# Attention and expert layer on one core: value products of neighbouring items side by side, three weight buffers, values projected at the end of the turn

## Chip, cores, metric

One NeuronCore of a Trainium2 chip. The metric is the device time of one execution, in microseconds (us). The profiler's names of the engines: PE is TensorE's matrix products (PEld its weight loads), DVE VectorE, ACT ScalarE, POOL GpSimd, SP the engine that issues DMAs here.

## What is computed

x has 16 batch items of 1024 tokens by 256. Attention has 16 heads of 16 dimensions, with rotary positions on q and k and a causal mask; then a gated mixture of 8 experts, the two best of each token.

```python
qkv = x @ W_qkv;  q, k, v = split(qkv);  q, k = rope(q, k)
att = einsum('bhtd,bhsd->bhts', q, k) / sqrt(16) + causal_mask
y = einsum('bhts,bhsd->bhtd', softmax(att), v) @ W_o
x = layernorm(x + y)
gate = softmax(x @ Wg + bg);  keep the two largest of 8, divide by their sum
out = layernorm(x + sum over experts of gate * (x @ We.T + be))
```

## The kernel before

The kernel works on one batch item per **turn**. Everything that a turn does is cut into steps, and one table, `ORDER`, writes all steps of a turn in a row; each engine runs its own part of each step in that order, and semaphores connect the engines. `plan(seg)` filters the table for five segments: `pre` (projection and first maxima of the first batch item), `first`, `mid` (14 turns), `last`, and `post` (the rest of the last item's expert layer). A middle turn does three things at once: attention of its own item, projection of the next item, expert layer of the item before.

- `ST.n.h`: scores of item n (0 to 47), head h of four, a bf16 product of up to 512 columns into one of NS = 3 PSUM tiles `scores` (line 963). ACT takes the exponential into `weights[:, n % 2]` (line 642). An *item* is one block of 128 keys by up to 512 queries for four heads; a slot of four heads has 12 items, whose widths are 512, 384, 256, 128 for the first four, then four of 512 and again 512, 384, 256, 128.
- `MASK.n`: on a diagonal item POOL sets weights above the diagonal to zero (line 559). 
- `PV.n`: the value product of item n. Four f32 products, one head each, with stationary values of 128 by 32; each goes to its own 32 partitions of `attend` (line 983). A f32 product stands in the trace as two passes, so one PV is eight records. PV.n stands after ST.n+1, since there are two weight buffers: the exponentials of item n+2 wait for PV.n (`attended`).
- `B.s.it.h`: the same scores the other way round, for the row maxima (line 947); DVE takes the maximum out of one of NB = 4 PSUM banks (lines 760, 763). `MC`, `MT` gather the maxima of a slot, which go by DMA into the stack for the next turn.
- `VP.j`: values of the next item for two token tiles (line 936), four steps a turn; ACT copies them into `v_next` (line 628). `VCOPY.s`: POOL copies slot s from `v_next` to `v_now` (line 584), when the slot's last value product is done.
- `XL`, `XT`: SP loads the next item's x in four pieces into `x_in` (line 472), PE transposes it (line 915). `QK`, `ROPE`, `CAST`, `LOAD` make the stacks of q and k.
- `YE`, `YT`, `HT`, `WO`: output of attention. `ZT`, `GL`, `GLT`, `GA`, `GB`, `GT`, `BE`, `MOE` (line 890): gating and experts; `BE.g.0`, `BE.g.1` are the products with the experts' bias (line 1045), whose contraction has 8 rows. `N1A`, `N2`, `R1`, `R2`, `N2A`: the norms; after `N2A` SP stores the result (line 518) and at the turn's end waits until the store has landed (line 522), before it issues `XL.0` of the next turn.

Of the kernel before, what the change touches and what calls it, by code (L numbers as in the profile page):

```python
# [38 lines left out]
NS = 3  # L39
DMA = 16  # L40
# [3 lines left out]
CONST_P, CONST_V = 4, 3  # L44
# [38 lines left out]
def item_work(n):  # L83
# [7 lines left out]
XL.0  # L91
ST.0.0 ST.0.1 ST.0.2 ST.0.3 XL.1 B.0.0.0 B.0.0.1 MC.3 B.0.0.2 B.0.0.3 MASK.0 PV.47 YE.3.1
ST.1.0 ST.1.1 B.0.1.0 ST.1.2 B.0.1.1 B.0.1.2 YT.3.1 ST.1.3 MASK.1 PV.0 B.0.1.3 B.0.2.0
ST.2.0 XT.0 B.0.2.1 XL.2 XT.1 B.0.2.2 ST.2.1 ST.2.2 XL.3 XR.0 ST.2.3 MASK.2 MT.3 B.0.2.3 PV.1
ST.3.0 ST.3.1 B.0.3.0 B.0.3.1 VCOPY.3 ST.3.2 ST.3.3 XR.1 MASK.3 B.0.3.2 PV.2
ST.4.0 ST.4.1 XT.2 XT.3 HT.0.0 HT.0.1 ST.4.2 ST.4.3 B.0.3.3 LOAD.0 B.0.4.0 B.0.4.1 PV.3 YE.0.0
ST.5.0 B.0.4.2 WO.0.0 WO.0.1 HT.1.0 HT.1.1 B.0.4.3 QK.0.0 ST.5.1 R1.0 ST.5.2 ST.5.3 WSPLIT B.0.5.0 B.0.5.1
  B.0.5.2 PV.4 ROPE.0.0
ST.6.0 B.0.5.3 B.0.6.0 B.0.6.1 ST.6.1 ST.6.2 ST.6.3 PV.5 B.0.6.2 B.0.6.3
ST.7.0 ST.7.1 B.0.7.0 B.0.7.1 CAST.0.0.0 QK.0.1 B.0.7.2 ST.7.2 CAST.0.0.1 ST.7.3 B.0.7.3 B.0.8.0 PV.6  # L100
ST.8.0 ROPE.0.1 N1A.0 WO.1.0 B.0.8.1 WO.1.1 ST.8.1 ST.8.2 ST.8.3 MASK.8 PV.7 B.0.8.2
ST.9.0 ST.9.1 B.0.8.3 B.0.9.0 CAST.0.1.0 QK.0.2 YT.0.0 B.0.9.1 ST.9.2 B.0.9.2 ST.9.3 MASK.9 R1.1 PV.8
# [52 lines left out]
def belongs(step, seg):  # L155
# [6 lines left out]
    if step in (("PV", SLOTS * ITEMS - 1), ("YE", SLOTS - 1, 1), ("YT", SLOTS - 1, 1)):  # L162
        return behind
# [925 lines left out]
```

## Time and profile before

| | |
|---|---|
| median of 3 runs | 3425.34 us (3417.21 to 3430.62) |
| the profiled execution's own time | 3433.1 us |
| its span | 3431.4 us |
| busy, share of the span | PE 96%, DVE 80%, ACT 55%, POOL 36% |
| mean granted TensorE clock | 0.975 of full |

The span is from the first to the last instruction. The 14 middle turns are alike, some 204.5 us each. Before them lie some 120 us of `pre` and the segment `first`, behind them `last` and some 110 us of `post`.

### The profile page before, as it was taken

What the parts mean: (1) busy time and instruction counts of PE and PEld (TensorE: products, weight loads), DVE (VectorE), ACT (ScalarE), POOL (GpSimd) and SP (SyncE); (2) the same over time, 40 slices, a digit from 0 to 9 for tenths busy, and PEclk for the clock granted to TensorE, in tenths of its full rate; (3) what the DMA queues carried; (4) which work ended last, traced back from release to release, by engine and by line L of the source; (5) the groups of instructions that cost most, each with busy time, mean ns of one, the idle gap of its engine ahead of it and who ended that gap; (6) DMA issues with size and microseconds to landing.
All of it is one profiled execution on the core that took longest, in us unless ns stands there. A gap on an engine that the chain in (4) does not pass through costs nothing.

```text
span 3431.4 us, 59169 instructions
## 1 busy us (share of the span) xinstructions
PE 3291.5 (96%) x19072; PEld 1738.4 (51%) x19072; DVE 2741.6 (80%) x8349; ACT 1897.2 (55%) x4257; POOL 1234.4 (36%) x1467
## 2 busy tenths in 40 slices
PE   5899999999999999999999999999999999999987
PEld 2234555555555555555555555555555555555555
DVE  5778887878888788888878888787888878888735
ACT  2367555564655556555564655657465564655541
POOL 4254324343333444334344332444334344432110
PEclk7799999999999999999999999999999999999998
DMA  5334343232433333343242433333343242434000
GB/s 135 59 61 81 52 84 56 45 79 48 83 52 68 59 58 70 52 84 57 50 79 42 83 57 74 57 55 69 58 78 57 52 75 50 77 52 72 2 25 13
DMA packets 174790, 210.98 MB, mean 61 GB/s; under 512 B 25992, under 2 KB 124560, under 8 KB 174224
## 3 DMA queue, kind: packets, MB, share of 16 engines
q1 hardware_dynamic: 173056, 202.98, 33.9%
q8 instruction: 153, 2.51, 0.4%
q10 hardware_dynamic: 1424, 4.21, 0.3%
q14 instruction: 157, 1.29, 0.2%
HBM read 138.43 MB, written 67.11 MB: 60 GB/s over the span
## 4 chain that ended last, share of the span: by engine, by line
PE 81%; DVE 9%; issue 3%; POOL 2%; DMA 2%; ACT 1%; DVEq 0%; ACTq 0%; SPq 0%; POOLq 0%
PE bank L890 22%; PE attend L983 15%; PE bank L947 13%; PE scores L963 13%; PE bank L927 6%; PE bank L1007 3%; PE bank L1045 2%; DVE bank L760 2%; PE bank L936 2%; DMA x_in<-in_x 2%; PE bank L991 1%; DVE maxima L763 1%; PE bank L915 1%; PE bank L998 1%; PE bank L1015 1%
## 5 line engine op out<-in xcount | busy, mean ns | idle before, releaser
L642 ACT ACTIVATE weights<-scores 128x512 f32<-128x512 f32 (+3 forms) x3072 | 1351.6, 494 | 1077.5 <-PE scores L963 1067.2
L760 DVE CUSTOM_DVE_ANT_0 bank<-bank,far_q 128x128 f32<-128x128 f32 (+3 forms) x2048 | 960.6, 514 | 217.2 <-PE bank L947 200.4
L963 PE MATMUL scores<-q_stack,k_stack 99*128 99x512 bf16 (+3 forms) x3072 | 826.1, 330 | 8.6 <-ACT weights L642 8.3
L947 PE MATMUL bank<-k_stack,q_stack 96*128 96x512 bf16 (+3 forms) x3072 | 792.6, 334 | 31.7 <-DMA k_stack<-parts_scratch 8.9
L559 POOL TENSOR_SCALAR_AFFINE_SELECT weights<-weights 128x512 f32<-128x512 f32 x512 | 325.3, 637 | 1201.7 <-ACT weights L642 1199.8
L763 DVE TENSOR_REDUCE maxima<-bank 128x1 f32<-128x512 f32 x1024 | 641.9, 682 | 49.0 <-PE bank L947 43.6
L983 PE MATMUL attend<-weights,v_now 128*32 128x512 f32 (+3 forms) x6144 | 660.9, 502 | 3.9 <-POOL weights L559 3.8
L963 PEld LDWEIGHTS scores<-q_stack,k_stack 99*128 99x128 bf16 x3072 | 265.7, 98 | 526.2 <-ACT weights L642 275.4
L947 PEld LDWEIGHTS bank<-k_stack,q_stack 96*128 96x128 bf16 x3072 | 271.2, 98 | 480.3 <-issue 242.2
L864 DVE SCALAR_TENSOR_TENSOR z<-bank,gates,z 128x256 f32<-128x256 f32 x512 | 247.0, 482 | 204.9 <-PE bank L890 203.6
L890 PE MATMUL bank<-wexp_hi,zT_hi 128*128 128x512 f32 x1024 | 377.2, 450 | 0.0
L890 PE MATMUL bank<-wexp_lo,zT_hi 128*128 128x512 f32 x1024 | 327.5, 401 | 0.0
L890 PE MATMUL bank<-wexp_hi,zT_lo 128*128 128x512 f32 x1024 | 325.9, 400 | 0.0
L927 PE MATMUL bank<-xT,wqkv_sb 128*128 128x512 f32 x512 | 248.4, 609 | 21.3 <-DVE z L866 13.9
L866 DVE SCALAR_TENSOR_TENSOR z<-bank,gates,z 128x256 f32<-128x256 f32 x512 | 247.9, 484 | 18.3
L983 PEld LDWEIGHTS attend<-weights,v_now 128*32 128x32 f32 x6144 | 121.6, 108 | 222.2 <-issue 171.9
L890 PEld LDWEIGHTS bank<-wexp_lo,zT_hi 128*128 128x128 f32 x1024 | 197.5, 193 | 47.3
L890 PEld LDWEIGHTS bank<-wexp_hi,zT_lo 128*128 128x128 f32 x1024 | 195.8, 191 | 47.4
L569 POOL TENSOR_SCALAR shrink<-moments 128x4 f32<-128x4 f32 x64 | 15.0, 234 | 561.2 <-DVE moments L878 388.9
L890 PEld LDWEIGHTS bank<-wexp_hi,zT_hi 128*128 128x128 f32 x1024 | 185.3, 196 | 53.6 <-issue 19.2
L548 POOL TENSOR_TENSOR rope<-rope,cos_sb 128x512 f32<-128x512 f32 x128 | 165.3, 1292 | 122.7 <-DVE rope_swap L789 122.6
L617 ACT ACTIVATE parts<-rope 128x512 bf16<-128x512 f32 x256 | 162.0, 633 | 60.5 <-POOL rope L552 30.8
(106 smaller groups left out, 3467.2 us busy)
## 6 DMA issues: line engine op xcount, KB each, us to landing
parts_scratch<-parts SPq DMA_DIRECT2D x128, 384.0 KB, 2.5
q_stack<-parts_scratch SPq DMA_DIRECT2D x384, 128.0 KB, 7.1
k_stack<-parts_scratch SPq DMA_DIRECT2D x384, 128.0 KB, 7.6
x_in<-in_x SPq DMA_DIRECT2D x64, 256.0 KB, 3.0
z<-in_x SPq DMA_DIRECT2D x32, 512.0 KB, 5.1
out<-z SPq DMA_DIRECT2D x32, 512.0 KB, 3.4
q_stack<-maxrow SPq DMA_DIRECT2D x192, 8.0 KB, 2.1
z<-in_w_exp ACTq DMA_DIRECT2D x1, 1024.0 KB, 14.5
```

The source lines that it names most:

```text
L548: pool.tensor_tensor(x1, x1, cos[:, ch * CH:(ch + 1) * CH], ALU.mult)
L559: pool.affine_select(out=block, in_=block, compare_op=ALU.is_ge, fill=no_weight, base=0, pattern=[[0, QUAD], [1, P]], channel_multiplier=- ...
L642: act.activation(weights[:, n % 2, hh, c0:CH], st[(QUAD * n + hh) % NS][:, c0:CH], ACT.Exp, scale=DH ** -0.5).then_inc(S["weights_ready"], 1)
L760: dve.tensor_tensor_reduce(out=b[:, 0:w], in0=b[:, 0:w], in1=far_q[:, CH - w:CH], scale=1.0, scalar=-SENTINEL, op0=ALU.add, op1=ALU.max, a ...
L763: dve.tensor_reduce(dst, b[:, 0:w], AX.X, ALU.max).then_inc(fr, 1)
L864: link(c, step, dve.scalar_tensor_tensor(out=acc, in0=b[:, 0:D], scalar=gates[:, t, 2 * ch:2 * ch + 1], in1=acc, op0=ALU.mult, op1=ALU.add))
L866: dve.scalar_tensor_tensor(out=acc, in0=b[:, D:2 * D], scalar=gates[:, t, 2 * ch + 1:2 * ch + 2], in1=acc, op0=ALU.mult, op1=ALU.add).then ...
L890: last = pe.matmul(dst, lhs(i, kt), rhs(j, kt), start=(i, j, kt) == pairs[0], stop=(i, j, kt) == pairs[-1])
L927: last = pe.matmul(b[:, :], wqkv[:, kt, col:col + P], xT[:, kt, ch * CH:(ch + 1) * CH], start=kt == 0, stop=kt == KT - 1)
L947: pe.matmul(b[:, 0:w], q_stack[0:ROWS, n, hh, qt * P:(qt + 1) * P], k_stack[0:ROWS, n, hh, kc * CH:kc * CH + w], start=True, stop=True).th ...
L963: pe.matmul(st[(QUAD * n + hh) % NS][:, c0:CH], k_stack[0:MROWS, s, hh, kb * P:(kb + 1) * P], q_stack[0:MROWS, s, hh, qc * CH + c0:(qc + 1 ...
L983: last = pe.matmul(pv[32 * j:32 * j + 32, c0:CH], v_now[:, s, o:o + 32], weights[:, n % 2, j, c0:CH], start=kb == 0, stop=kb == 4 * qc + 3)
```

## The change

Three buffers hold weights (`NW = 3`), so PV.n may stand one item later; the table puts PV.2m and PV.2m+1 next to each other, after ST.2m+2 and the mask. `v_next` and `v_now` become one tile `values` of five places. Slots 0 to 2 of the next item are projected straight into the places 1 to 3 that the products read, and slot 3 into place 4, from which POOL copies it to place 0 (one copy a turn in place of four). So VP can run only when slots 0 to 2 have been used: it stands at ST.45 to ST.47, at the end of the turn. The last two value products of an item (46, 47) run in the next turn, before only the last one did. Two small tiles of the gating are reused in place. The table of all steps is written anew; two lines of it before and after:

```diff
+NW = 3
-ST.15.0 ST.15.1 ST.15.2 GT.0 VP.3 ST.15.3 CAST.0.3.0 MASK.15 B.1.2.2 PV.14 B.1.2.3 B.1.3.0
-ST.16.0 ST.16.1 BE.0.0 ST.16.2 ST.16.3 B.1.3.1 CAST.0.3.1 B.1.3.2 B.1.3.3 PV.15 YE.1.0
+ST.15.0 B.1.2.1 MT.0 ST.15.1 ST.15.2 BE.0.0 BE.0.1 B.1.2.2 MOE.0.0.0 ST.15.3 B.1.2.3 B.1.3.0 MASK.15
+ST.16.0 ST.16.1 MOE.0.0.1 CAST.0.3.0 ST.16.2 B.1.3.1 B.1.3.2 MOE.0.0.2 B.1.3.3 ST.16.3 PV.14 PV.15 YE.1.0
...
-    if step in (("PV", SLOTS * ITEMS - 1), ("YE", SLOTS - 1, 1), ("YT", SLOTS - 1, 1)):
+    if step in (("PV", SLOTS * ITEMS - 2), ("PV", SLOTS * ITEMS - 1), ("YE", SLOTS - 1, 1), ("YT", SLOTS - 1, 1)):
...
-        v_next = sb("v_next", [P, SLOTS, VQ])
-        v_now = sb("v_now", [P, SLOTS, VQ])
+        values = sb("values", [P, SLOTS + 1, VQ])
-        weights = sb("weights", [P, 2, QUAD, CH])
+        weights = sb("weights", [P, NW, QUAD, CH])
...
                 elif kind == "VCOPY":
-                    (s,) = a
-                    if s < SLOTS - 1:
-                        emptied(pool, c, ("VP", TILES // 2 - 1))
-                    if c.seg != "pre" and (c.seg != "first" or s < SLOTS - 1):
-                        pool.wait_ge(S["attended"], c.at("attended", ("PV", ITEMS * s + ITEMS - 1)))
+                    projected(pool, c)
+                    if c.seg != "first":
+                        pool.sem_inc(S["pool_waits"], 1)
+                        pool.wait_ge(S["attended"], c.at("attended", ("PV", SLOTS * ITEMS - 1)))
                     pool.sem_inc(S["pool_waits"], 1)
-                    pool.tensor_copy(v_heads(v_now, s), v_heads(v_next, s)).then_inc(S["values_copied"], 1)
+                    pool.tensor_copy(v_heads(0), v_heads(SLOTS)).then_inc(S["values_copied"], 1)
...
                         act.wait_ge(S["values_copied"], c.at("values_copied", ("VCOPY", SLOTS - 1)))
+                        act.wait_ge(S["attended"], c.at("attended", ("PV", ITEMS * (SLOTS - 1) - 1)))
...
-                        if n >= 2:
-                            act.wait_ge(S["attended"], c.at("attended", ("PV", n - 2)))
+                        if n >= NW:
+                            act.wait_ge(S["attended"], c.at("attended", ("PV", n - NW)))
...
-                        last = pe.matmul(pv[32 * j:32 * j + 32, c0:CH], v_now[:, s, o:o + 32],
-                                         weights[:, n % 2, j, c0:CH], start=kb == 0, stop=kb == 4 * qc + 3)
+                        last = pe.matmul(pv[32 * j:32 * j + 32, c0:CH], values[:, (s + 1) % SLOTS, o:o + 32],
+                                         weights[:, n % NW, j, c0:CH], start=kb == 0, stop=kb == 4 * qc + 3)
```

What PE runs in a middle turn around the bias products `BE` (line 1045; 1047 after), before:

```order
L1045 MATMUL bank<-narrow 128x256 x2
L963 MATMUL scores<-q_stack,k_stack 128x512 x2
L947 MATMUL bank<-k_stack,q_stack 128x512 x3
L983 MATMUL attend<-weights,v_now 32x128 x4
L963 MATMUL scores<-q_stack,k_stack 128x512
L947 MATMUL bank<-k_stack,q_stack 128x512
L963 MATMUL scores<-q_stack,k_stack 128x512
L947 MATMUL bank<-k_stack,q_stack 128x512
L963 MATMUL scores<-q_stack,k_stack 128x512
L1045 MATMUL bank<-narrow 128x256 x2
L890 MATMUL bank<-wexp_hi,zT_hi 128x512 x2
```

and with the change:

```order
L963 MATMUL scores<-q_stack,k_stack 128x256 x2
L947 MATMUL bank<-k_stack,q_stack 128x384
L985 MATMUL attend<-weights,values 32x512 x4
L985 MATMUL attend<-weights,values 32x384 x4
L963 MATMUL scores<-q_stack,k_stack 128x128
L947 MATMUL bank<-k_stack,q_stack 128x384
L953 MATMUL bank<-ident,maxima 32x128
L963 MATMUL scores<-q_stack,k_stack 128x128 x2
L1047 MATMUL bank<-narrow 128x256 x4
```

The two bias products stand together (x4), no longer with eight rows between them, and the row of value products (line 985 after) is a pair, 512 and 384 wide, where before each stood alone between other products.

What PE runs at the passage from one turn to the next (line 915 is XT, the transposition of the x that SP loads; lines 983 and 985 are the value products), before, from PV.46 on:

```order
L983 MATMUL attend<-weights,v_now 32x256 x4
L963 MATMUL scores<-q_stack,k_stack 128x512 x4
L947 MATMUL bank<-k_stack,q_stack 128x128 x4
L983 MATMUL attend<-weights,v_now 32x128 x4
L963 MATMUL scores<-q_stack,k_stack 128x384 x2
L947 MATMUL bank<-k_stack,q_stack 128x256
L963 MATMUL scores<-q_stack,k_stack 128x384
L947 MATMUL bank<-k_stack,q_stack 128x256 x2
L991 MATMUL bank<-ident,head_out 128x128 x4
L963 MATMUL scores<-q_stack,k_stack 128x384
L983 MATMUL attend<-weights,v_now 32x512 x4
L947 MATMUL bank<-k_stack,q_stack 128x256
```

and with the change, from the last value projection (VP.3, line 936) on:

```order
L936 MATMUL bank<-wqkv_sb,xT 128x256 x4
L963 MATMUL scores<-q_stack,k_stack 128x128 x2
L947 MATMUL bank<-k_stack,q_stack 128x512
L915 MATMUL bank<-ident,x_in 128x128 x8
L947 MATMUL bank<-k_stack,q_stack 128x128 x2
L963 MATMUL scores<-q_stack,k_stack 128x512 x2
L947 MATMUL bank<-k_stack,q_stack 128x128 x2
L947 MATMUL bank<-k_stack,q_stack 128x256 x2
L963 MATMUL scores<-q_stack,k_stack 128x512 x2
L947 MATMUL bank<-k_stack,q_stack 128x256
L985 MATMUL attend<-weights,values 32x256 x4
L985 MATMUL attend<-weights,values 32x128 x4
```

The first transposition of the next item's x stood further down, among the scores of the third item; now it is the first thing of the turn, behind the value projections.

In a middle turn the step table has 24 pairs of value products. Of these 23 follow each other on PE with nothing between; PV.18 and PV.19 have maxima products between them.

## Rows read from the trace of the kernel before

**Rows 1.** The page: busy time, share of the span, instructions of each engine.

```profile
PE 3291.5 (96%) x19072; PEld 1738.4 (51%) x19072; DVE 2741.6 (80%) x8349; ACT 1897.2 (55%) x4257; POOL 1234.4 (36%) x1467
```

**Rows 2.** The page: the chain that ended last, by engine and by line.

```profile
PE 81%; DVE 9%; issue 3%; POOL 2%; DMA 2%; ACT 1%; DVEq 0%; ACTq 0%; SPq 0%; POOLq 0%
PE bank L890 22%; PE attend L983 15%; PE bank L947 13%; PE scores L963 13%; PE bank L927 6%; PE bank L1007 3%; PE bank L1045 2%; DVE bank L760 2%; PE bank L936 2%; DMA x_in<-in_x 2%; PE bank L991 1%; DVE maxima L763 1%; PE bank L915 1%; PE bank L998 1%; PE bank L1015 1%
```

**Rows 3.** Windows: length, busy us (instructions), clock, DMA; one turn, then two short stretches.

```profile
core 0: us, PE busy (x) PEld busy (x) DVE busy (x) ACT busy (x) POOL busy (x), PEclk, DMA share, GB/s
1511.03:1715.50 204.47, 201.82 (x1196) 107.79 (x1192) 169.57 (x521) 118.36 (x267) 77.67 (x92) 0.99 0.37 63
1658.99:1662.40 3.41, 3.41 (x17) 1.84 (x16) 2.98 (x8) 0.66 (x3) 0.63 (x1) 1.00 0.03 5
1662.40:1665.80 3.40, 3.40 (x16) 2.06 (x15) 2.03 (x7) 2.92 (x7) 2.72 (x3) 0.50 0.02 5
```

**Rows 4.** Waits of PE, 300 to 3200 us: total us, times, longest.

```profile
PE bank L927 <- DVE z L866: 13.9, 14, 1.0
PE bank L1037 <- DVE gates L849: 12.5, 14, 0.9
PE scores L963 <- ACT weights L642: 4.7, 16, 0.7
PE bank L915 <- DMA x_in<-in_x: 3.8, 8, 0.8
```

**Rows 5.** Timeline of PE around one group of value products (start us, us, line).

```profile
1499.85 0.82 PE L963 MATMUL scores<-q_stack,k_stack 99*128 99x512 bf16 x3
1500.60 0.64 PE L983 MATMUL attend<-weights,v_now 128*32 128x512 f32 x4
...
1501.06 0.61 PE L983 MATMUL attend<-weights,v_now 128*32 128x512 f32 x4
1501.60 0.39 PE L963 MATMUL scores<-q_stack,k_stack 99*128 99x512 bf16 x1
1501.83 0.38 PE L947 MATMUL bank<-k_stack,q_stack 96*128 96x512 bf16 x1
```

**Rows 6.** Timeline of PEld, the same stretch.

```profile
1499.85 0.33 PEld L963 LDWEIGHTS scores<-q_stack,k_stack 99*128 99x128 bf16 x3 [0.28 <-issue]
1500.60 0.16 PEld L983 LDWEIGHTS attend<-weights,v_now 128*32 128x32 f32 x8 [0.42 <-issue]
1501.60 0.10 PEld L963 LDWEIGHTS scores<-q_stack,k_stack 99*128 99x128 bf16 x1 [0.84 <-ACT weights L642]
```

**Rows 7.** Timeline of PE around the two bias products of one half.

```profile
1659.22 0.22 PE L963 MATMUL scores<-q_stack,k_stack 99*128 99x128 bf16 x1
1659.38 1.13 PE L1045 MATMUL bank<-narrow 8*128 8x256 f32 x4
1660.43 0.60 PE L947 MATMUL bank<-k_stack,q_stack 96*128 96x512 bf16 x2
1660.88 0.22 PE L963 MATMUL scores<-q_stack,k_stack 99*128 99x128 bf16 x1
1661.03 1.13 PE L1045 MATMUL bank<-narrow 8*128 8x256 f32 x4
```

**Rows 8.** Page and timeline: the end of a turn, out of ACT and SP.

```profile
1505.87 2.08 ACT L676 ACTIVATE z<-z,shrink 128x256 f32<-128x256 f32 x4
...
1507.97 0.40 SPq L518 DMA_DIRECT2D out<-z  x1
1511.03 7.86 SPq L472 DMA_DIRECT2D x_in<-in_x  x4
...
x_in<-in_x SPq DMA_DIRECT2D x64, 256.0 KB, 3.0
```

**Rows 9.** Groups of PE by line: busy us, mean ns (value projection).

```profile
L936 PE MATMUL bank<-wqkv_sb,xT 128*128 128x256 f32 x512 | 121.4, 381 | 4.6 <-ACT rope L607 3.3 <-ACT v_next L628 0.9 <-DVE maxima_hi L760 0.5
```

**Rows 10.** Timeline of DVE from the gates' first step to the last.

```profile
1567.77 0.28 DVE L834 MAX8 top<-logits 128x8 f32<-128x8 f32 x3
...
1572.90 0.19 DVE L849 TENSOR_TENSOR gates<-chosen,gate_sum 128x32 f32<-128x32 f32 x1
```

**Rows 11.** Timeline of SP at the start of the first item.

```profile
119.63 1.77 SPq L510 DMA_DIRECT2D q_stack<-maxrow  x3
121.44 6.01 SPq L472 DMA_DIRECT2D x_in<-in_x  x4
```

**Rows 12.** The page: groups of ACT and DVE that feed or free PE.

```profile
L642 ACT ACTIVATE weights<-scores 128x512 f32<-128x512 f32 (+3 forms) x3072 | 1351.6, 494 | 1077.5 <-PE scores L963 1067.2
L760 DVE CUSTOM_DVE_ANT_0 bank<-bank,far_q 128x128 f32<-128x128 f32 (+3 forms) x2048 | 960.6, 514 | 217.2 <-PE bank L947 200.4
...
L763 DVE TENSOR_REDUCE maxima<-bank 128x1 f32<-128x512 f32 x1024 | 641.9, 682 | 49.0 <-PE bank L947 43.6
```

More of the change, by code:

```diff
@@ L146 @@
[L146 to L151 removed]
+XL.0 XL.1 XT.0 XL.2 XT.1 XL.3 B.0.0.0 B.0.0.1 MC.3
@@ L195, in plan @@
                 out += [("LOAD", 1)]
-        out += [("VCOPY", s) for s in range(SLOTS - 1)]
         out += [("LOAD", 2)] + scores + [("MC", 0), ("MT", 0)]
@@ L413, in attention_moe_kernel, with v_heads, projected @@
         free = [sem(f"bank{i}_free") for i in range(NB)]
-        def v_heads(buf, s):
-            return buf[:, s, 0:TILES * QUAD * VW].rearrange("p (b h v) -> p b h v", b=TILES, h=QUAD)
+        def v_heads(place):
+            return values[:, place, 0:TILES * QUAD * VW].rearrange("p (b h v) -> p b h v", b=TILES, h=QUAD)
+        def projected(eng, c):
+            before = {"first": ("pre",), "last": ("mid", NMID - 1)}.get(c.seg)
+            if c.seg == "mid":
+                before = ("mid", c.turn - 1) if c.turn else ("first",)
+            emptied(eng, Count(*before), ("VP", TILES // 2 - 1))
         def filled(eng, c, step):
@@ L557, in work @@
                     pool.wait_ge(S["weights_ready"], c.at("weights_ready", ("ST", n, QUAD - 1)))
-                    block = weights[:, n % 2, :, c0:c0 + P]
+                    block = weights[:, n % NW, :, c0:c0 + P]
                     pool.affine_select(out=block, in_=block, compare_op=ALU.is_ge, fill=no_weight, base=0,
@@ L845, in work @@
                     dve.wait_ge(S["gate_exp"], c.at("gate_exp", ("GA", a[0])))
-                    link(c, step, dve.tensor_tensor(chosen[:, :, :], gate_e[:, :, :], picked[:, :, :], ALU.mult))
-                    link(c, step, dve.tensor_reduce(gate_sum[:, 0], chosen[:, :, :], AX.X, ALU.add))
+                    link(c, step, dve.tensor_tensor(picked[:, :, :], shift[:, :, :], picked[:, :, :], ALU.mult))
+                    link(c, step, dve.tensor_reduce(gate_sum[:, 0], picked[:, :, :], AX.X, ALU.add))
                     link(c, step, dve.reciprocal(gate_sum[:, 1], gate_sum[:, 0]))
-                    dve.tensor_tensor(gates[:, :, :], chosen[:, :, :],
+                    dve.tensor_tensor(gates[:, :, :], picked[:, :, :],
                                       gate_sum[:, 1].unsqueeze(2).to_broadcast([P, 4, NE]), ALU.mult) \
@@ L970, in work @@
                     c0 = score_width(kb, qc)
-                    if it == 0:
+                    if n == 0:
+                        projected(pe, c)
+                    elif n == ITEMS * (SLOTS - 1):
                         pe.wait_ge(S["values_copied"], c.so_far("values_copied", step))
```

131 lines of the change are left out of this document (62 added, 69 removed).

## Prediction

> **What bounds the kernel.** I read the page's first part, then its chain, then one middle turn, then PE's waits, and last the single records. TensorE is busy 96% of the span, no other engine over 80% [rows 1], and the chain that ended last lies on it for 81%, 15% on the value products alone [rows 2]. A middle turn lasts 204.47 us, of which PE is busy 201.8; VectorE 169.6 and ScalarE 118.4 [rows 3]. From 300 to 3200 us PE's named waits come to under 30 us in all, two of which come once a turn: 1.0 us for a bank that VectorE frees late (13.9 us) and 0.9 us for the gates (12.5 us) [rows 4]. So only what shortens PE's own stream shortens the kernel, and "busy" hides one thing: what PE loses between products.
>
> That loss shows in the starts [rows 5]. Three score products start at 1499.85, and in an undisturbed stream each next 512-wide one starts 0.22 later (1501.60 to 1501.83 is 0.23). So the third starts at about 1500.29, and the value product behind it at 1500.60, 0.31 later: 0.09 lost on entering. Inside the group the second pass starts 0.46 after the first. From the second pass to the next score product it is 0.54: 0.08 lost on leaving. The weight loads tell the same [rows 6]: three score weights are loaded within 0.33, ahead of their products, but the first load for the value product starts only at 1500.60, with the product, and the next full-width load only at 1501.60. Each change between full-width products and 32-column products costs PE 0.08 to 0.09 us.
>
> **The pairs.** Before, each of the 768 value products is entered and left alone. The new order puts 23 pairs a turn together, 16 times: 368 passages from a value product to a full-width one and back are gone. The trace has no passage from one item's value product to the next item's (the price of it is unknown); the nearest row is the passage between the two passes of one group, 0.46, which has the same kind of product, the same 32-column places and a fresh load of weights each time [rows 5, 6]. If the passage between items is like it, a pair saves 0.09 + 0.08 = 0.17 us. The other end is a passage that drains as the outer ones do: 0. Below 0 nothing speaks, as the second item now waits for weights that are an item older. I take 0.175, since the starts are rounded and the sum of the two may be 0.17 or 0.18: 368 x 0.175 = **64 us** (bounds 0 and 66).
>
> **The bias products.** They have the same kind of loss: a 128-wide score product (0.06 in a stream) starts at 1659.22 and the bias product at 1659.38, 0.10 late, and leaving is much like it [rows 7]. Two of them a half now stand together, in two halves of 16 turns: 32 x 0.18 = **6 us** (bounds 0 and 6).
>
> **Waits that go or come.** The 1.0 us wait for VectorE stood at a projection whose bank the expert product before it had used while VectorE was busy with a row of maxima; in the new order this projection (QK.1.1) has a pair of value products and a maxima product between it and the last user of its bank, 2 us of cover: **-14 us** (bounds 0 and 14). The gates: VectorE needs 5.3 us from the first step to the last, 1567.77 to 1573.09 [rows 10]. In the new order some 4 us of PE work lie between GA and the transposition GT, with two maxima products that VectorE takes in between, and VectorE starts GA about as PE comes to it; so PE waits again, 5.3 - 4 = 1.3 to 1.4 us in place of 0.9: **+5 us** (bounds -12 and +15).
>
> **x at the head of the turn.** The transposition XT.0 is now the first work of a turn. What it needs: ScalarE's last normalization, 2.08 us, the store of its result, from issue to the next load's issue 3.06 us, and the load, 3.0 us to landing [rows 8]. The normalization now stands behind the first exponential of item 46, say 0.8 us after PE began that item; with it the data is there 8.9 us after the first score product of item 46. Between the two points PE now has three value projections (121.4 us / 64 = 1.9 each, 5.7) [rows 9], a pair of value products (1.0 as in [rows 5], and some 0.8 for one of 384 columns), and at 0.22 for 512 columns eight narrow score products (0.7) and ten maxima products (1.6): 9.8 us. So it is just covered, and I cost it at nothing in a middle turn; what hides it is those three projections, and if they moved, up to 5 us a turn would show. Before, XT.1 waited already, 3.8 us in all [rows 4]. At the very first turn there is no cover: x is loaded from 121.44 on [rows 11], so PE stands until about 124.5 where it had work before, though later waits for the same loads go: **+3 us** (bounds 0 and 6).
>
> **Edits at nothing.** Three buffers of weights cost no time by themselves: ScalarE waits 1067 us in all for scores [rows 12], and since PE runs ST.n+3 behind PV.n anyway, its wait for `attended` is over before the scores are there. Three copies fewer lie on GpSimd, which is busy 36%. The projections' copies on ScalarE at the turn's end fall in its idle time. SP passes nothing new except two residual loads that it issues earlier. GA's exponential in place adds no step. POOL's mask of the second item of a pair stands right before the pair, as before; its cover is the first item's up to 1.0 us.
>
> **The clock.** Once in most turns the granted clock falls to 0.50, its lower level of 1.2 GHz, for 3.4 us; the stretch before had it at 1.00 and holds both bias products of a half [rows 3, 7]. At half speed 3.4 us of work lose 1.7 us. With the bias products now side by side in both halves of a turn, and next to a pair of value products in one, I expect a second such stretch in some turns: 5 x 1.7 = **+9 us** (bounds: -20, all of them gone, and +71, three more a turn).
>
> **The sum** against the profiled execution: -64 - 6 - 14 + 5 + 3 + 9 = -67, 3433.1 to 3366. The median of the runs shown lies 7.8 us below that execution; from 3425.34 the forecast is **3358 us**. Half a percent, 17 us, is about what a measurement of this kernel can tell from no change.
>
> **Rivals.**
> Weights are not loaded ahead across items. A value product of the next item may find its loads held until the pass in flight is over; one load takes 0.11 us, and eight of them overlap within 0.16 [rows 6]. Then a pair keeps about 0.11 of the loss and saves 0.065: 368 x 0.065 = 24 in place of 64, which gives 3398. Against it: the second pass's loads stand already within the 0.16 at the group's start, while the first pass streams. The Trainium skill (TensorE: Matmul & The Clock Gate, Part 3) says that a weight load overlaps products in flight only when its row group differs, and all value products use all rows; by that rule the gain would be this smaller one, but the rows of before do not bear it out. Chance 7%.
>
> The clock takes it back. If pairs of 32-column products and neighbouring bias products bring three more half-speed stretches a turn, 14 x 3 x 1.7 = 71 us go: 3420, no change; two more give 3396. For it: the one fall there is follows bias products. Against: no fall follows the value products elsewhere in a turn, where they take 15% of the chain. [...] Chance 11%.
>
> The passage between two items drains like any other: the pairs save nothing, and the sum is -6 - 14 + 5 + 3 + 9: 3422, no change. Only the absence of any row for it speaks for it. Chance 6%.
>
> VectorE falls behind, and it is slower. During a pair PE feeds VectorE nothing for 1.9 us. A turn has 200 - 169.6 = 30 us of slack on VectorE, 1.3 us for each of the 23 pairs. Four banks hold at most four maxima of 0.5 to 0.68 us [rows 12], 2.0 to 2.7 us of work, if they are full when the pair starts. If they are mostly empty and VectorE idles 1.6 us a pair, it needs 169.6 + 23 x 1.6 = 206.4 us a turn and bounds it: 14 x (206.4 - 204.5) = 27 us and the first and last turn 4, so 3456. It decides from 1.3 us of idleness a pair on. Against: in the table three or four maxima products often stand right before a pair. Chance 6%.
>
> **Chances.** Forecast 70%, the rivals 7, 11, 6 and 6. Faster by over 0.5% (under 3408): 70 + 7 + about 5 of the clock's 11 (fewer than three more stretches) = 82%. Within: the other 6 and 6 of the clock and the draining passage: 12%. Slower: 6%. The range reaches down by the gate and clock bounds, 12 and 14 of them, to 3332, and up to 3408, which takes in the rule's 3398 and the clock's two stretches, and leaves out the last two rivals and the clock's full price.
>
> **What would show it.** In the changed kernel: two neighbouring groups of a pair with 0.46 from pass to pass, also across the items (0.55 or more would be the draining rival); a turn of about 200 us; PE's named waits without line 927 and still with the gates; transposition at the turn's head without a wait over 0.5 us; one or two half-speed stretches a turn. Wrong: a turn over 203 us, waits of PE for maxima of over 1 us a pair, or the clock below 0.96.

## The result, and the profile after

The changed kernel takes **3327.57 us** (median of 4 runs, 3321.81 to 3333.02), the kernel before in the same series 3427.37 (4 runs). The ratio is 0.9713 with a 95% interval of 0.9691 to 0.9734: faster by 100 us, and 98 below the 3425.34 that the forecast started from, where 67 were forecast. The predicted time, 3358, was 30 us too high, and the result lies 4 us below the range, which ended at 3332. The profiled execution took 3333.0, its span 3331.3 at a mean clock of 0.969; a later one of the same kernel had a span of 3317.8 at 0.975.

The page, the busy line that answers to [rows 1]:

```profile
PE 3209.5 (96%) x19072; PEld 1791.1 (54%) x19072; DVE 2690.4 (81%) x8349; ACT 1888.8 (57%) x4257; POOL 1212.4 (36%) x1418
```

PE is the bound as before, with the same 19072 products, and is busy 82 us less. (The chain of waits, [rows 2], is followed back over less than a third of this span, so I don't use it.) Of the groups of the page, the value products are those that gave most:

```profile
L985 PE MATMUL attend<-weights,values 128*32 128x512 f32 (+3 forms) x6144 | 582.3, 494 | 1.0 <-POOL weights L559 0.9
```

Before, the same 6144 records had 660.9 us of busy time (mean 502). The window of one middle turn, from one load of x to the next, against [rows 3]:

```profile
core 0: us, PE busy (x) PEld busy (x) DVE busy (x) ACT busy (x) POOL busy (x), PEclk, DMA share, GB/s
1474.20:1670.81 196.61, 195.63 (x1194) 110.81 (x1193) 165.88 (x521) 118.04 (x266) 76.31 (x89) 0.99 0.38 66
```

196.61 us in place of 204.47, PE busy 195.63 in place of 201.82. PE's idle time has gone from 2.65 to 0.98 us, and VectorE, for about the same work, is busy 3.7 us less. That second fact is the first that the forecast had nothing for. PE's waits from 300 to 3200 us, against [rows 4]:

```profile
PE bank L915 <- ACT values L628: 6.1, 12, 0.5
PE scores L963 <- ACT weights L642: 2.3, 7, 0.5
...
PE bank L915 <- DMA x_in<-in_x: 1.0, 1, 1.0
```

Line 927's wait for z is gone, as forecast. The wait for the gates is gone too, which was not forecast. New is line 915, the transposition at the turn's head, which waits 0.5 us a turn for ScalarE's copies of the projected values; its data from SP is in time. Now one pair of value products on PE, pass by pass:

```profile
1502.95 1.03 PE L947 MATMUL bank<-k_stack,q_stack 96*128 96x512 bf16 x4
1503.91 0.64 PE L985 MATMUL attend<-weights,values 128*32 128x512 f32 x4
...
1504.36 1.04 PE L985 MATMUL attend<-weights,values 128*32 128x512 f32 x8
...
1504.79 1.04 PE L985 MATMUL attend<-weights,values 128*32 128x512 f32 x8
...
1505.22 0.61 PE L985 MATMUL attend<-weights,values 128*32 128x512 f32 x4
1505.77 0.61 PE L947 MATMUL bank<-k_stack,q_stack 96*128 96x512 bf16 x2
```

(A pass is four records; where a line says x8 it holds two passes.) The four passes start at 1503.91, 1504.36, 1504.79 and 1505.22: 0.45, 0.43, 0.43 apart. It is the same everywhere: in all 110 pairs of 512-wide items at full clock the passages are 0.453, 0.429 and 0.429 us and the exit to the next product 0.545, each within 0.002; in the 381 lone 512-wide groups of before 0.453 and 0.545, within 0.003. The passage between the items, 1504.36 to 1504.79, is no longer than that inside an item, and inside the second item the passage is 0.02 to 0.03 shorter than the 0.46 of [rows 5]. The weight loads of the same pair, against [rows 6]:

```profile
1503.91 0.16 PEld L985 LDWEIGHTS attend<-weights,values 128*32 128x32 f32 x8 [0.35 <-issue]
1504.37 0.13 PEld L985 LDWEIGHTS attend<-weights,values 128*32 128x32 f32 x4 [0.30 <-ACT weights L642]
1504.80 0.13 PEld L985 LDWEIGHTS attend<-weights,values 128*32 128x32 f32 x4 [0.30 <-issue]
```

The loads for the second item's passes (1504.79 and 1505.22) start at 1504.37 and 1504.80, each as the pass before starts, across the items too.

### The profile page after: what moved, and what is told of

Same layout as the page of the kernel before. It is cut to its first block and busy times, and to the rows that moved or that the text cites. A ratio compares the mean times of both kernels' runs of the same rounds, so it can differ in the third digit from the quotient of the medians.

```text
span 3331.3 us, 59099 instructions
## 1 busy us (share of the span) xinstructions
PE 3209.5 (96%) x19072; PEld 1791.1 (54%) x19072; DVE 2690.4 (81%) x8349; ACT 1888.8 (57%) x4257; POOL 1212.4 (36%) x1418
## 3 DMA queue, kind: packets, MB, share of 16 engines
q1 hardware_dynamic: 173056, 202.98, 34.9%
## 5 line engine op out<-in xcount | busy, mean ns | idle before, releaser
L642 ACT ACTIVATE weights<-scores 128x512 f32<-128x512 f32 (+3 forms) x3072 | 1336.3, 494 | 959.8 <-PE scores L963 950.7
L947 PE MATMUL bank<-k_stack,q_stack 96*128 96x512 bf16 (+3 forms) x3072 | 811.8, 336 | 36.8 <-DVE maxima L763 9.6
L985 PE MATMUL attend<-weights,values 128*32 128x512 f32 (+3 forms) x6144 | 582.3, 494 | 1.0 <-POOL weights L559 0.9
L963 PEld LDWEIGHTS scores<-q_stack,k_stack 99*128 99x128 bf16 x3072 | 280.8, 98 | 419.0 <-ACT weights L642 155.3
L947 PEld LDWEIGHTS bank<-k_stack,q_stack 96*128 96x128 bf16 x3072 | 278.9, 99 | 413.8 <-issue 162.4
L890 PE MATMUL bank<-wexp_hi,zT_hi 128*128 128x512 f32 x1024 | 389.4, 462 | 0.1
L985 PEld LDWEIGHTS attend<-weights,values 128*32 128x32 f32 x6144 | 158.6, 109 | 287.1 <-issue 229.5
L453 POOL TENSOR_TENSOR parts<-rope,parts 128x512 bf16<-128x512 f32 x120 | 140.5, 1171 | 215.1 <-ACT parts L616 215.1
L451 POOL TENSOR_TENSOR rope<-rope,parts 128x512 f32<-128x512 f32 x120 | 139.2, 1160 | 175.4 <-ACT parts L616 175.4
```

Source lines behind the costliest of these rows:

```text
L642: act.activation(weights[:, n % NW, hh, c0:CH], st[(QUAD * n + hh) % NS][:, c0:CH], ACT.Exp, scale=DH ** -0.5).then_inc(S["weights_ready"], 1)
L890: last = pe.matmul(dst, lhs(i, kt), rhs(j, kt), start=(i, j, kt) == pairs[0], stop=(i, j, kt) == pairs[-1])
L947: pe.matmul(b[:, 0:w], q_stack[0:ROWS, n, hh, qt * P:(qt + 1) * P], k_stack[0:ROWS, n, hh, kc * CH:kc * CH + w], start=True, stop=True).th ...
L963: pe.matmul(st[(QUAD * n + hh) % NS][:, c0:CH], k_stack[0:MROWS, s, hh, kb * P:(kb + 1) * P], q_stack[0:MROWS, s, hh, qc * CH + c0:(qc + 1 ...
L985: last = pe.matmul(pv[32 * j:32 * j + 32, c0:CH], values[:, (s + 1) % SLOTS, o:o + 32], weights[:, n % NW, j, c0:CH], start=kb == 0, stop= ...
```

## Experiments

Each kernel was timed against the kernel before on the same chip. Differences from the changed kernel are taken to its second timing: 3323.99 us (3319.57 to 3330.75), ratio 0.9701 (0.9687 to 0.9716). It ran on the same chip as experiments 5 to 7. Experiments 1 to 4 ran on another, where the kernel before took 3422.34 us (17 runs) in place of 3425.77 (9 runs); by the ratios experiments 1 and 4 are 73 and 45 us slower than the changed kernel, 2 more than the differences below, and such a difference is good to some 7 us. Durations of a turn are means over 13 turns, from the first issue of `out<-z` to the 27th (two a turn). "Stretches" are the pieces of 3.4 us with the granted clock at 0.50, counted between these two issues. The time that a kernel lost to the clock is given as (1 - mean clock) x time, which is what its work would have taken less at full clock throughout.

### 1. The pairs taken apart

```diff
+def split_pairs(order):
+    out = list(order)
+    for n in range(0, SLOTS * ITEMS, 2):
+        i = out.index(("PV", n + 1))
+        if out[i - 1] != ("PV", n):
+            continue
+        j = next(j for j in range(i + 1, len(out)) if out[j][0] in ("ST", "B"))
+        out.insert(i, out.pop(j))
+    return out
+ORDER = split_pairs(ORDER)
```

In the changed kernel one score or maxima product from behind each pair is put between its two items. All else stays. The reverse, pairs in the kernel before, was not run.

> The changed kernel with one full-width product (the next score or maxima product) taken from behind each pair of value products and put between its two items; 23 pairs a turn, 368 in all. Theory A: each pair saves an entry (0.09), an exit (0.10) and what the second item no longer loses at its own passages (its first pass follows 0.429 us after the pass before it and its second pass again 0.429, where a lone item's second pass follows after 0.453), in all 0.23 us: the kernel is slower than the changed one by 368 x 0.23 = 86 us, 3414 us, faster than before by 0.4%. Theory B (the price in the prediction, 0.175 a pair): slower by 64 us, 3392. Theory C (the gain is in the new order's waits, not in the pairs): slower by under 30 us, under 3358.

3395.06 us, ratio 0.9915 (0.990 to 0.993): 71 us slower than the changed kernel. The edit reached 318 of the 368 pairs (where a step of another engine stands in the table between the items, it passed them by), so one pair is worth 71 / 318 = **0.22 us** (0.20 to 0.25 with the uncertainty of 7 us), and Theory A, scaled to 318 pairs 74 us, holds; B would give 56, which lies outside. A pair that was taken apart:

```profile
1586.23 0.38 PE L978 MATMUL scores<-q_stack,k_stack 99*128 99x512 bf16 x1
1586.54 1.07 PE L1000 MATMUL attend<-weights,values 128*32 128x512 f32 x8
1587.54 0.45 PE L962 MATMUL bank<-k_stack,q_stack 96*128 96x128 bf16 x4
1587.92 1.07 PE L1000 MATMUL attend<-weights,values 128*32 128x512 f32 x8
...
```

Each group alone costs 1.00 us from its start to the next product (1586.54 to 1587.54). Side by side the two cost 1503.91 to 1505.77, 1.86, and one entry of 0.09 less: 2.00 + 0.09 - 1.86 = 0.23.

### 2. GpSimd's rotation away from the gates, in the kernel before

```diff
-ST.14.0 ROPE.0.3 ST.14.1 ST.14.2 VP.1 GA.0 GB.0 ST.14.3 VP.2 MASK.14 PV.13 B.1.2.1 MT.0
+ST.14.0 ST.14.1 ST.14.2 VP.1 GA.0 GB.0 ST.14.3 VP.2 MASK.14 ROPE.0.3 PV.13 B.1.2.1 MT.0
```

Why VectorE's part of the gates had become short shows in single records. Before:

```profile
1568.16 1.11 DVE L836 TENSOR_TENSOR shift<-logits,top 128x32 f32<-128x32 f32 x1
1569.19 1.29 DVE L838 COPY taken<-top 128x8 f32<-128x8 f32 x1
```

and on GpSimd, the rotation of q and k, at the same time:

```profile
1567.95 1.27 POOL L548 TENSOR_TENSOR rope<-rope,cos_sb 128x512 f32<-128x512 f32 x1 [1.49 <-DVE rope_swap L789]
1569.18 1.27 POOL L549 TENSOR_TENSOR rope_swap<-rope_swap,sin_sb 128x512 f32<-128x512 f32 x1
```

A subtraction of 32 elements a partition and a copy of 8 last over a microsecond, 2.0 us more than below in all, and each ends within 0.05 us of GpSimd's step beside it (1569.27 and 1569.22; 1570.48 and 1570.45). The same two in the changed kernel, with nothing on GpSimd beside them:

```profile
L836 DVE TENSOR_TENSOR shift<-logits,top x32: 191/192/194, 338.9 to 3287.9; 128x32 f32<-128x32 f32 x32
L838 DVE COPY taken<-top x32: 164/165/167, 339.0 to 3288.1; 128x8 f32<-128x8 f32 x32
```

(ns, least / median / most of 32). In the changed kernel the gates begin on VectorE at 1526.87 and end with the first of these rows, 3.5 us later in place of the 5.3 of [rows 10]; PE comes to their transposition behind that:

```profile
1530.20 0.19 DVE L849 TENSOR_TENSOR gates<-picked,gate_sum 128x32 f32<-128x32 f32 x1
```

```profile
1530.71 0.60 PE L1039 MATMUL bank<-ident,gates 128*8 128x128 f32 x4
```

With 1.8 us more on VectorE PE would wait about 1.5 us (1530.39 + 1.8 against 1530.71), near the 1.3 to 1.4 forecast. To test whether the rotation, and not the new order around `GT`, makes the wait, it alone was moved in the kernel before.

> The kernel before with the rotation ROPE.0.3 moved in the table from ahead of the gates' steps GA.0 and GB.0 to behind MASK.14. Theory A: PE's wait for the gates (1.05 us a turn) comes from GpSimd's rotation, which runs beside VectorE's small steps from SBUF and stretches them from 0.2 to 0.6-1.3 us; without it GA and GB take 3.5 instead of 5.3 us and the wait goes: 14 to 15 us faster than before (3413), line 836 at 0.19 us in every turn. Theory B: the wait is one of distance between GB and GT on PE alone: no change of the time, VectorE's span of 5.3 us stays.

3403.48 us, ratio 0.9943 (0.9929 to 0.9956): 19 us faster than the kernel before, by a move of one step. That step holds GpSimd's rotation and, ahead of it, a shuffle of 0.73 us on VectorE (line 789), so two things have left the gates. VectorE now takes 3.6 us for them (1553.47 to 1557.09) in place of 5.3, and starts them 0.5 us sooner after their input. PE's wait was 0.9: the 1.7 us cover it alone, the shuffle's 0.5 would not. PE's waits, 300 to 3200 us:

```profile
PE bank L927 <- DVE z L866: 13.9, 14, 1.0
PE scores L963 <- ACT weights L642: 4.7, 16, 0.7
...
PE bank L1037 <- DVE gates L849: 0.9, 1, 0.9
```

The gates' wait fell from 12.5 us to 0.9, and every record of line 836 stood at 191 to 193 ns. The other 7 us fit the clock: the profiled execution had 5 stretches at half speed where the kernel before had 10 to 12 in three executions (below), and 6 x 1.2 to 1.7 = 7 to 10. It was no accident of one execution: the mean granted clock was 0.976 to 0.979 in all six runs of this kernel (median 0.9775) and 0.973 to 0.977 in the 17 of the kernel before on this chip (median 0.975). Why the order after the move has fewer stretches no run shows.

### 3. The same at the wait for z, in the kernel before

```diff
-ST.25.0 QK.1.0 B.2.1.0 B.2.1.1 ST.25.1 YT.1.1 ST.25.2 ST.25.3 MASK.25 B.2.1.2 PV.24 VCOPY.0 VCOPY.1 ROPE.1.0
+ST.25.0 QK.1.0 B.2.1.0 B.2.1.1 ST.25.1 YT.1.1 ST.25.2 ST.25.3 MASK.25 B.2.1.2 PV.24 VCOPY.0 VCOPY.1
...
-ST.27.0 MT.1 MOE.0.2.3 MOE.0.3.0 ST.27.1
+ST.27.0 MT.1 ROPE.1.0 MOE.0.2.3 MOE.0.3.0 ST.27.1
```

At that place, too, GpSimd's rotation stands beside VectorE, which writes the row of maxima:

```profile
1622.88 0.27 DVE L777 CAST maxrow<-bank 32x128 bf16<-32x128 f32 x1
...
1623.50 1.05 DVE L780 CAST maxrow<-maxrow_err 32x128 bf16<-32x128 f32 x1
1624.58 1.38 DVE L781 TENSOR_TENSOR maxrow<-maxrow_err,maxrow 32x128 bf16<-32x128 f32 x1
```

```profile
1621.94 1.28 POOL L548 TENSOR_TENSOR rope<-rope,cos_sb 128x512 f32<-128x512 f32 x1
1623.18 1.29 POOL L549 TENSOR_TENSOR rope_swap<-rope_swap,sin_sb 128x512 f32<-128x512 f32 x1
1624.55 1.28 POOL L552 TENSOR_TENSOR rope<-rope,rope_swap 128x512 f32<-128x512 f32 x1
```

Line 777 reads PSUM and takes its ordinary 0.27 beside GpSimd; lines 780 and 781 read SBUF and take 1.05 and 1.38 (0.21 and 0.28 with nothing on GpSimd).

> The kernel before with the rotation ROPE.1.0 moved in the table from the end of item 25's row to behind MT.1. Theory A: the 1.0 us wait of PE for a bank at QK.1.1 comes from VectorE's two small steps of MT.1 (lines 780, 781) that run beside GpSimd's rotation and take 1.05 and 1.38 us; apart from it they take 0.2 and 0.3 and the wait goes: 14 us faster than before. Theory B: the bank is late because of VectorE's row of maxima: no change. Against both a new wait can come: ScalarE's cast of the rotated tile now follows it more closely.

3420.43 us, ratio 0.9993 (0.9983 to 1.0003): no change, which is Theory B's time, but with Theory A's mechanism.

```profile
PE bank L1037 <- DVE gates L849: 13.4, 15, 1.0
PE bank L890 <- ACT rope L607: 6.7, 14, 0.6
```

The 13.9 us of line 927 are gone, as expected, and half of them came back at once as a wait of the next expert product for ScalarE. So the stall was GpSimd's doing as well, but in this kernel its removal bought nothing that the whole time shows. The 13 turns did get shorter, 2644.4 us against 2655.9 to 2661.1 in three executions of the kernel before, and two to four fewer half-speed stretches are 2 to 7 of it; the time ahead of the first store got longer, 440.8 against 430.8 to 436.7.

### 4. and 5. The bias products apart

First with much between them:

```diff
-B.1.2.0 MASK.14 PV.12 PV.13
-ST.15.0 B.1.2.1 MT.0 ST.15.1 ST.15.2 BE.0.0 BE.0.1 B.1.2.2
+B.1.2.0 MASK.14 BE.0.0 PV.12 PV.13
+ST.15.0 B.1.2.1 MT.0 ST.15.1 ST.15.2 BE.0.1 B.1.2.2
...
-B.2.9.0 ST.33.2 ST.33.3 MASK.33
-ST.34.0 B.2.9.1 YT.2.0 BE.1.0 BE.1.1 ST.34.1
+B.2.9.0 BE.1.0 ST.33.2 ST.33.3 MASK.33
+ST.34.0 B.2.9.1 YT.2.0 BE.1.1 ST.34.1
```

> The changed kernel with the two bias products of each half apart again: BE.0.0 ahead of the pair PV.12, PV.13, and BE.1.0 ahead of the last two score products of item 33. Theory A: four changes of array shape a turn come back (0.09 each, 0.37 a turn, 6 us), and nothing else: 3334. Theory B: side by side they bring the second half-speed stretch of a turn (16 such stretches in the 13 turns from 429 to 2993 us against 13 before, alternating between the two halves); apart the one of the first half goes, some 7 stretches x 1.7 = 12 us, net 6 us faster: 3322.

3366.75 us, ratio 0.9832 (0.9818 to 0.9847): 43 us slower than the changed kernel. It tells little of shapes, since `BE.g.0` now came too early:

```profile
PE bank L1047 <- ACT narrow L690: 21.4, 29, 0.9
```

Half of the 43 us is this wait. Much of the other half is the clock: the 13 turns of this execution held as much half-speed time as 22 stretches of 3.4 us, the most of all kernels here, and the mean clock of its five runs was 0.967 to 0.969. Neither theory holds: not A, whose "nothing else" fails, and not B, since the stretches became more. So the pair was taken apart again with one product between:

```diff
-ST.15.0 B.1.2.1 MT.0 ST.15.1 ST.15.2 BE.0.0 BE.0.1 B.1.2.2
+ST.15.0 B.1.2.1 MT.0 ST.15.1 ST.15.2 BE.0.0 B.1.2.2 BE.0.1
...
-ST.34.0 B.2.9.1 YT.2.0 BE.1.0 BE.1.1 ST.34.1
+ST.34.0 B.2.9.1 YT.2.0 BE.1.0 ST.34.1 BE.1.1
```

> The changed kernel with one product between the two bias products of each half (BE.0.0 B.1.2.2 BE.0.1 and BE.1.0 ST.34.1 BE.1.1), nothing moved further. Unlike e4 no bias product comes nearer to the gates' copy that it waits for. Theory A: two more changes of array shape a half, 0.18 to 0.2 us, 32 halves: 6 us slower than the changed kernel, and the half-speed stretches as many as in it (16 from 429 to 2993 us). Theory B: the half-speed stretches become fewer, and the kernel as fast as the changed one or faster.

3346.07 us, ratio 0.9763 (0.975 to 0.9776): 22 us slower than the changed kernel, and no new wait. The shapes are part of it. A bias product alone takes 1.06 us to the next product:

```profile
1615.13 1.13 PE L1047 MATMUL bank<-narrow 8*128 8x256 f32 x4
1616.19 0.28 PE L963 MATMUL scores<-q_stack,k_stack 99*128 99x256 bf16 x1
1616.40 1.12 PE L1047 MATMUL bank<-narrow 8*128 8x256 f32 x4
1617.46 0.32 PE L947 MATMUL bank<-k_stack,q_stack 96*128 96x256 bf16 x1
```

two side by side in the changed kernel 1.92:

```profile
1533.82 1.99 PE L1047 MATMUL bank<-narrow 8*128 8x256 f32 x8
1535.74 0.34 PE L947 MATMUL bank<-k_stack,q_stack 96*128 96x384 bf16 x1
```

With an entry of 0.1 less that is 2.12 + 0.1 - 1.92 = 0.3 a pair, about 9 us for 32. The rest is the clock: this execution had 19 stretches, those of the changed kernel 16, 6 and 5, and the mean clock was 0.966 to 0.969 in its five runs (median 0.967) against 0.969 to 0.975 in nine of the changed kernel (median 0.972). The lower clock is 17 us more lost; since eleven stretches of 1.7 us lost went with 13.5 us of time (below, 1.2 each), 17 lost are 12 to 17 us of time. Neither theory holds: A had 6 us and no more stretches, B fewer. The half-speed stretch behind the products above (columns as in the window above):

```profile
1617.60:1621.00 3.40, 3.40 (x10) 2.43 (x10) 1.64 (x5) 1.26 (x3) 0.00 (x0) 0.50 0.69 235
```

The stretch at 1.2 GHz again follows bias products. I had feared that standing side by side brings more of them; in this order of steps it is standing apart that goes with more. It is no rule, for they stood apart in the kernel before too, which has fewer stretches than either.

### 6. The transposition at the head of the turn two items later

```diff
-XL.0 XL.1 XT.0 XL.2 XT.1 XL.3 B.0.0.0 B.0.0.1 MC.3
-ST.0.0 ST.0.1 B.0.0.2
+XL.0 XL.1
+ST.0.0 ST.0.1 XT.0 XL.2 XT.1 XL.3 B.0.0.0 B.0.0.1 MC.3 B.0.0.2
```

> The changed kernel with the first two score products of a turn ahead of the first transposition of the next item's x (and of the loads after it). PE waits there 0.5 us a turn for ScalarE's copies of the last value projection, not for the load. Theory A: with two score products (0.43 us) ahead the wait goes: 14 x 0.5 = 7 us faster than the changed kernel. Theory B: the load itself is the next to be late, or the copy waits as long behind ScalarE's exponentials: no change.

3327.17 us, ratio 0.971 (0.9696 to 0.9723): the same as the changed kernel, as Theory B has it. The wait of line 915 for `values` is gone, and in its place stand

```profile
PE scores L963 <- ACT weights L642: 6.8, 19, 0.5
PE bank L947 <- ACT xT L599: 6.7, 25, 0.5
```

My reading, which no run isolates: ScalarE is what is short there, since the copies of values and of the transposed x come between exponentials, and whichever PE asks for first is late.

### 7. Three value products together

```diff
+def in_threes(order):
+    out = list(order)
+    for s in range(SLOTS):
+        for a in (4, 7):
+            n = ITEMS * s + a
+            for m in range(n, n + 3):
+                out.remove(("PV", m))
+            i = out.index(("ST", n + 3, 2))
+            out[i:i] = [("PV", m) for m in range(n, n + 3)]
+    return out
+ORDER = in_threes(ORDER)
```

> The changed kernel with value products in threes where the item's accumulation allows it: in each slot 0 1, 2 3, 4 5 6, 7 8 9, 10 11, still with three weight buffers; a three stands ahead of the third score product of the next item, whose exponentials wait until its first value product is done. Theory A (what counts is the number of groups of value products): 25 groups a turn become 20, 5 x 0.23 x 16 = 18 us faster than the changed kernel. Theory B: ScalarE, held back by the full weight buffers, delays score products by more than that: slower, with PE waiting for line 642 by over 1 us a slot.

3550.82 us, ratio 1.036 (1.0346 to 1.0374): 227 us slower than the changed kernel, many times what a passage side by side can be worth. A turn went from 196 to 211 us. PE's largest waits:

```profile
PE scores L979 <- ACT weights L658: 24.6, 54, 1.0
PE bank L963 <- DVE maxima_hi L776: 21.7, 29, 1.4
...
```

and one turn:

```profile
1502.10:1714.10 212.00, 202.63 (x1193) 112.11 (x1192) 165.48 (x520) 117.53 (x268) 76.61 (x90) 0.98 0.35 61
```

On PE the run of three itself is as cheap as hoped:

```profile
1640.92 2.78 PE L1001 MATMUL attend<-weights,values 128*32 128x512 f32 x24
1643.64 0.39 PE L979 MATMUL scores<-q_stack,k_stack 99*128 99x512 bf16 x1
```

2.72 us for six passes, which is 0.45, four times 0.43 and 0.55 for the last with its exit. But three buffers hold only three items' weights, so while a three waits to run ScalarE has nowhere to write: its exponentials wait 400 us for value products from 300 to 3200 us (110 waits), where in the changed kernel no such wait is among its six largest. And while the three lasts PE feeds neither ScalarE nor VectorE. What comes behind it waits: in the window 9.4 us of idle a turn in place of 1.0, more of it for VectorE (lines 776, 779 and 882: 50 us over the 14 turns) than for line 658 (24.6 us), and the wait for the gates is back (12.8). Neither theory has this: A's 18 us faster is refuted, and B has the sign but not the place, since it wanted over 1 us a slot for ScalarE and 24.6 us are 0.4. Over the 13 turns, 211.3 us each against 196.1, idle is 8.5 of the 15.1 us. Counting each product from its start to the next one's with the idle left out, the 192 maxima products of a turn take 3.7 us longer, the 192 score products 2.3, and no other group over 0.6; at most 1.6 of this is the clock. So the remainder lies with the products that wait for the other engines, in time that the profile counts as busy.

### 8. to 10. Both kernels again

> The kernel before once more, one look. Theory A: the number of half-speed stretches in the 13 middle turns is not a property of the kernel but differs between executions, as 16 and 6 did for the changed kernel; then this execution need not show one per turn (13), and its span moves by 1.7 us for each stretch more or fewer. Theory B: the stretches follow from the order of PE's work; then there are 13 again, 204.8 us apart, and the span is 3431 us within 3.

> The kernel before a third time. Theory A (differs between executions): a number of half-speed stretches that may be anything from some 6 to 19. Theory B (set by the order): 13 again. If both looks give 13, the stretches of the kernel before are fixed and only those of the changed kernel vary.

> The changed kernel a third time. Theory A: another number of half-speed stretches in the middle turns than 16 or 6, and a span of 3317.8 us plus 1.7 us for each stretch beyond 6, so 3334.8 us at 16. Theory B: 6 or 16 again. What it decides: whether the difference of 10 to 15 us between two executions of the changed kernel is the clock's alone.

The kernel before: 10 and 11 stretches, after 12 in the first profile (a 13th, which the expectations count, lies on the first store); spans 3425.4 and 3425.5 against 3431.4. So its number is not fixed either, as Theory A has it, though it varies little. The changed kernel: 5 stretches and a span of 3317.9, after 16 (3331.3) and 6 (3317.8, the profile of the second timing). Theory A for the changed kernel: eleven stretches more and 13.5 us more, 1.2 us for each, less than the 1.7 that it had.

The mean clock of every run says more than these few profiles: 0.973 to 0.977 in 26 runs of the kernel before (median 0.975), 0.969 to 0.975 in nine of the changed one (median 0.972). That is 86 us lost to the clock before, 93 with the change.

## Why the prediction was right in its sign and too small

Two steps of the prediction failed, each a term of its sum. The price of a pair, "0.09 + 0.08 = 0.17 us", was too small: 0.22 to 0.23 was measured, 20 us more over 368 pairs. And the gates' wait, put at +5 because VectorE's 5.3 us were taken as work, came out at -12.5, 17 us more. With either of them put right the forecast would have been 3338 or 3341, 10 to 13 us above the measured time. The range went down 26 us from the forecast; the bounds of its own terms allowed 51, to 3307.

The gain is best counted a turn. From two executions with few stretches, the issues of the first and the 27th store, in the kernel before (c1) and the changed one:

```profile
433.51 0.38 SPq L518 DMA_DIRECT2D out<-z  x1
...
3089.40 0.38 SPq L518 DMA_DIRECT2D out<-z  x1
```

```profile
429.57 0.38 SPq L519 DMA_DIRECT2D out<-z  x1
2979.41 0.38 SPq L519 DMA_DIRECT2D out<-z  x1
```

2655.9 us against 2549.8, 106 us in 13 turns, of which four stretches fewer (6 against 10) are 5 to 7: **7.6 us a turn**. The terms, forecast and found:

| term | forecast, us a turn | found, us a turn |
|---|---|---|
| pairs | -4.0 (64 over 16 turns) | -5.2 (23 x 0.22 to 0.23) |
| bias products | -0.4 | -0.6 |
| wait for z | -1.0 | -1.0 |
| wait for the gates | +0.4 | -0.9 |
| x at the turn's head | 0 | +0.2 (0.5 for `values`, less 0.3 for x) |
| sum | -5.0 | -7.5 |

**The pairs**: the mechanism was right, the size wrong. The forecast took the passage between items as equal to the 0.46 inside a group, and the step "a pair saves 0.09 + 0.08" counted only the two passages that go. The trace of the changed kernel has 0.43 for both passages behind the first, and leaving cost 0.12 (0.545 less 0.429): 0.09 + 0.12 + 0.02 for the second item's inner passage is 0.23 in place of 0.175, 17 to 20 us in all. The upper bound of 66 was therefore none: it took the row of a group's first passage for the least that a passage can be, and that first passage is slower than all later ones of the same run. The rival that weights are not loaded ahead is refuted by the 0.43 and by experiment 1. By that rule (the Trainium skill, TensorE: Matmul & The Clock Gate, Part 3, in its list of what overlaps: a load overlaps products in flight only when its row group differs) a pair would have saved 0.065; the trace doesn't agree, with loads of the same 128 rows starting 0.42 us ahead of their pass. The same section of the Trainium skill also lets a load into the background weight buffer go ahead of products in flight, and the trace fits that.

**The gates** are the step that failed in sign. "VectorE needs 5.3 us from the first step to the last" was taken as work; 2.0 us of it were lines 836 and 838 standing still beside GpSimd. The rows that say so were in the trace of before: line 836 with 0.19 us in 18 of its 32 records and 1.11 us at this place. The forecast cost what lies between `GA` and `GT` on PE and never asked what GpSimd does then. The bound of -12 was on hand; -12.5 came. The 4 us that it put between GA and GT on PE were right: 3.84 (1526.87 to 1530.71). The Trainium skill (SBUF — State Buffer, Who interferes with whom) states it: VectorE and GpSimd share a pair of ports under an exclusive lock, and an operation of VectorE with at most one SBUF input outside the two-port modes doesn't contend. The traces agree: line 836 (two SBUF inputs) ends with GpSimd's step, lines 777 (PSUM) and 841 (one SBUF input, 0.16 us beside GpSimd and apart from it) do not wait. Lines 838 and 780, a copy and a cast with one SBUF input, wait too; the Trainium skill lists both kinds among those that can run in a two-port mode, and no row here shows in which mode they ran. In the changed kernel the lock still costs such steps their time, line 781 1.37 to 1.40 us in 15 of its 64 records, but not where PE waits for them.

**The wait for z** went as forecast, 14 us, but my reason, "VectorE was busy with a row of maxima", stopped halfway: lines 780 and 781 of that row took 1.9 us longer beside GpSimd (experiment 3).

**The head of the turn.** The three projections cover the load, as forecast: one wait for x, 1.0 us, in place of eight. What the sum didn't have is that these same projections give ScalarE two copies just ahead of the transposition, 0.5 us a turn. In experiment 6 two score products ahead of the transposition bought nothing: the wait moved to other products.

**The clock** was forecast at +9 with bounds of -20 and +71. Found: 5 to 16 stretches in 13 turns against 10 to 12, so -10 to +7 us depending on the execution; in the medians of all runs, 0.972 against 0.975, 7 us lost, 5 to 7 us of time. The size was near, but not for the reason given: experiment 5 speaks against neighbouring bias products, and some 5 us of the loss lie behind the 27th store, in the last turns and `post` (28 us against 22 to 24), which the term did not cover. What sets the number of stretches stays open.

**The rest.** Ahead of the first store and behind the 27th the two kernels differ by 1.5 us only, where three more turns' worth of pairs should give 16. What stands against them is PE's idle time ahead of the first store, 69.5 us in place of 54.5. Waits for x are 3.4 of these 15 us (+3 was forecast): one of 6.0 at the head of the first turn, to 124.96, less what later ones lost. From there to the first store PE also waits 5 us longer for VectorE's maxima and 3 us longer for line 642; the sum had nothing for these. At the end the clock takes 3 to 5 (0.77 in place of 0.82 over 110 us of `post`), while PE's idle time there is 4 us less.

One reading of a row was off without harm: the four waits of [rows 4] come to 34.9 us, not "under 30"; the two that were costed are 26.4 of them.

The forecast's signs to look for: 0.46 or less from pass to pass across items, yes (0.43); a turn of about 200 us, lower (197); line 927 without a wait, yes; "still with the gates", no; transposition at the head under 0.5 us, at the limit (0.5); one or two half-speed stretches a turn, only in the first profile (16 in 13 turns, then 6 and 5). That VectorE falls behind, the rival on the slow side, did not come with pairs; experiment 7 shows where it and ScalarE do, at three.

## What to carry to other kernels

Count changes of array shape on PE: putting two 32-column products side by side was worth 0.22 us each time, though the page called PE 96% busy in both kernels, and three in a row, with buffers for three, made the kernel 125 us slower than before. When a short step of VectorE stands in a chain that PE waits for, compare that record with the median of its line, and if it is five times longer look at what GpSimd does in that microsecond: moving that one rotation was worth 19 us here, 12 of them the wait; the rest fits the clock. A stall removed is worth nothing until it is known what is late next (experiments 3 and 6).

## What the runs showed of the hardware that was not expected

- Some steps of VectorE that read only SBUF stand still until GpSimd's step is over, 0.19 us becoming 1.11, 0.17 becoming 1.29, 0.21 becoming 1.05, 0.28 becoming 1.38: tensor-tensor steps with two inputs in SBUF, a copy and a cast. Others that read only SBUF keep their time beside GpSimd: MATCH_REPLACE8 0.16 us (line 841), the norms' statistics 0.43 (line 813). Steps with an input in PSUM keep theirs.
- The first passage between passes of 32-column products takes 0.453 us, each later one of the same run 0.429, in pairs and in threes, across items as inside one.
- The number of half-speed stretches is no constant of a kernel: 16, 6 and 5 in 13 turns of the changed one. Eleven more of them went with 13.5 us more, 1.2 us each, as much in all as many a change is worth. One rotation of GpSimd's moved (experiment 2), and six runs out of six had a clock of 0.976 or more.
